# All D groups ahead of c1, and q weights of chunks 0 to 3 made by VectorE, in a three-layer interaction kernel

## The reference

```
z    = einsum('bid,bjd->bdij', base, curr)
curr = einsum('bdij,ijh->bhd', z, W_k) + b_k      # 100 outputs each
```

## Time and profile before

| | |
|---|---|
| device time, median of 3 runs | 185.86 us (185.47 to 185.96) |
| profiled execution: its time, its span from first to last instruction | 186.29 us, 184.5 us |
| PE matmul busy | 175.8 us (95% of the span) |
| DVE busy | 151.8 us (82%) |
| ACT busy | 73.9 us (40%) |
| POOL busy | 16.2 us (9%) |
| DMA moved | 37.71 MB, mean 204 GB/s |

### The profile page before, as it was taken

How to read it: one execution, slowest core, us unless ns; L and a number is a source line. 1 busy time by engine, 2 the same in 40 slices (tenths; PEclk the granted TensorE clock), 3 DMA queues, 4 the chain that set the end, 5 groups by cost and what they waited for, 6 DMA issues and landing times.

```text
span 184.5 us, 2573 instructions
## 1 busy us (share of the span) xinstructions
PE 175.8 (95%) x814; PEld 118.7 (64%) x814; DVE 151.8 (82%) x135; ACT 73.9 (40%) x79; POOL 16.2 (9%) x21
## 2 busy tenths in 40 slices
PE   7798998869999999999999999999999999999994
PEld 2364474546677777777777777777777777777760
DVE  0699698869999999999999999999999999300622
ACT  2554664124444624462446244534453445002001
POOL 3670010087000000000000000000000000000000
PEclk9999999999999999999999999999999999999999
DMA  6999997999797739774986597659765200000000
GB/s 192 379 409 411 412 219 218 231 406 397 230 324 233 234 122 321 247 227 124 331 230 228 126 322 235 223 135 329 228 219 128 99 0 0 0 0 4 0 0 0
DMA packets 11845, 37.71 MB, mean 204 GB/s; under 512 B 2305, under 2 KB 2941, under 8 KB 11838
## 3 DMA queue, kind: packets, MB, share of 16 engines
q1 hardware_dynamic: 11538, 37.38, 62.1%
q0 software_dynamic: 48, 0.16, 0.3%
q10 hardware_dynamic: 252, 0.09, 0.3%
HBM read 36.28 MB, written 1.33 MB: 204 GB/s over the span
## 4 chain that ended last, share of the span: by engine, by line
PE 79%; DMA 8%; SPq 3%; POOL 3%; issue 2%; DVE 1%; ACT 1%; DVEq 0%; ACTq 0%
PE q_ps L434 39%; PE c_ps L434 36%; DMA pair_sb<-d_dram 3%; DMA pair_sb<-w_pairs 3%; DMA d_dram<-w_d 2%; PE q_ps L518 2%; SPq L153 2%; POOL pair_sb L401 1%; POOL wq_low L424 1%; PE q_ps L443 1%; POOL wc_low L406 1%; DVE xb_z L246 1%; ACT z_high L324 1%; SPq L159 1%; PE c_ps L565 1%
## 5 line engine op out<-in xcount | busy, mean ns | idle before, releaser
L324 ACT ACTIVATE z_high<-xb_z 126x1024 fp32r<-126x1024 f32 x56 | 59.2, 1060 | 73.0 <-DVE xb_z L246 69.3
L253 DVE TENSOR_TENSOR z_low<-xb_z,z_high 126x1024 fp32r<-126x1024 f32 x56 | 68.9, 1232 | 1.1 <-ACT z_high L324 0.8
L246 DVE TENSOR_TENSOR xb_z<-x_a,xb_z 126x1024 f32<-126x1024 f32 x50 | 62.1, 1242 | 8.3 <-DMA xb_z<-xw 8.3
L434 PE MATMUL q_ps<-z_high,wq_high 126*101 126x512 f32 x108 | 34.1, 396 | 3.0 <-POOL wq_low L424 1.5
L434 PE MATMUL c_ps<-z_high,wc_high 126*101 126x512 f32 x112 | 35.5, 398 | 0.2 <-issue 0.2
L434 PE MATMUL c_ps<-z_high,wc_low 126*101 126x512 f32 x112 | 35.0, 394 | 0.0
L434 PE MATMUL c_ps<-z_low,wc_high 126*101 126x512 f32 x112 | 35.0, 394 | 0.0
L434 PE MATMUL q_ps<-z_high,wq_low 126*101 126x512 f32 x108 | 33.8, 394 | 0.0
L434 PE MATMUL q_ps<-z_low,wq_high 126*101 126x512 f32 x108 | 33.7, 393 | 0.0
L434 PEld LDWEIGHTS q_ps<-z_high,wq_high 126*101 126x101 f32 x108 | 17.7, 165 | 10.8 <-POOL wq_low L424 2.0
L434 PEld LDWEIGHTS c_ps<-z_high,wc_high 126*101 126x101 f32 x112 | 18.0, 165 | 9.0 <-issue 1.6
(11 more groups left out here) (56 smaller groups left out, 66.1 us busy)
## 6 DMA issues: line engine op xcount, KB each, us to landing
xb_z<-xw SPq DMA_DIRECT2D x50, 512.0 KB, 4.5
x_a<-xa SPq DMA_DIRECT2D x8, 512.0 KB, 5.0
w_d<-w2h SPq DMA_DIRECT2D x4, 512.0 KB, 7.4
w_post<-w1x SPq DMA_DIRECT2D x3, 512.0 KB, 10.0
d_dram<-w_d SPq DMA_DIRECT2D x4, 252.5 KB, 4.3
w_post<-w1x SPq DMA_DIRECT2D x1, 562.5 KB, 12.7
pair_sb<-d_dram SPq DMA_DIRECT2D x6, 82.9 KB
pair_sb<-w_pairs SPq DMA_DIRECT2D x1, 404.0 KB, 5.4
```

The costliest lines, as they stand in the source:

```text
L246: nc.vector.tensor_tensor(xb_z[0:K, c, :], x_a[0:K, u % 2, :], x_b, ALU.mult).then_inc(z_done, 1)
L253: nc.vector.tensor_tensor(z_low[0:K, m % SLOTS, :], xb_z[0:K, c, :], z_high[0:K, m % SLOTS, :].bitcast(fp32), ALU.subtract).then_inc(low_d ...
L324: nc.scalar.activation(z_high[0:K, m % SLOTS, :], xb_z[0:K, m % C, :], ACT.Copy).then_inc(high_done, 1)
L434: last = nc.tensor.matmul(ps[0:J, h * B:(h + 1) * B], w[0:K, c * J:(c + 1) * J], z[0:K, slot, h * B:(h + 1) * B], start=(c == 0 and k == 0 ...
```

## The change

PE does D groups 0 and 1, then `select_xb(6)`, then groups 2, 3 and 4, and all c1 chunks from 1 on after that. DVE copies groups 1 and 3 out of PSUM (around form(5)), ACT groups 0, 2 and 4. DVE makes the q weights of chunks 0 and 1 after split(9) of step m = 10, and those of chunks 2 and 3 after split(11) of step m = 12; POOL makes those of chunks 4 to 6 alone, on semaphores of its own. SP issues `load_xb(1, 2)` behind the gathers of piece 0 and `load_xb(1, 3)` behind all gathers.

```diff
-PREP_AT = 9
+PREP_AT = (10, 12)
...
@@ sync
-            sp.wait_ge(dgroup_copied, 2)
+            sp.wait_ge(dgroup_copied, 1)
+            sp.wait_ge(dgroup_copied_dve, 1)
...
-            sp.wait_ge(dgroup_copied, 4)
+            sp.wait_ge(dgroup_copied, 2)
+            sp.wait_ge(dgroup_copied_dve, 2)
...
-            sp.wait_ge(dgroup_copied, NG)
+            sp.wait_ge(dgroup_copied, 3)
             store_d(sp, 0, LEFT + 4 * GI, 4 * GI, LOWER - 4 * GI, d_stored)
-            sp.wait_ge(low_done, 3)
-            load_xb(1, 2)
             sp.wait_ge(equals_cleared, 1)
             sp.wait_ge(d_stored, 16 * DS)
             sp.wait_ge(d_stored_pool, 16)
             for side, t, piece in GATHER:
                 if piece == 1 and (side, t) == (0, 0):
-                    sp.wait_ge(low_done, 4)
-                    load_xb(1, 3)
+                    sp.wait_ge(low_done, 3)
+                    load_xb(1, 2)
                 if side == 0 or piece > 0:
                     gather_d(sp, side, t, piece)
-            for c in range(4, C):
+            for c in range(3, C):
                 sp.wait_ge(low_done, c + 1)
                 load_xb(1, c)
@@ vector
+            def copy_d(g):
+                dve.wait_ge(dgroup_done, g + 1)
+                nc.vector.tensor_copy(w2_d[:, g * GI * J:(g + 1) * GI * J], d_ps[g % 2]).then_inc(dgroup_copied_dve, 1)
+
-            def first_weights():
+            def first_weights(i):
...
                 for m in range(m0, m0 + BODY):
+                    if m == 5:
+                        copy_d(1)
                     form(it, m)
+                    if m == 5:
+                        copy_d(3)
...
-                    if m == PREP_AT:
-                        first_weights()
                     if m > 1:
                         split(it, m - 1)
+                    if m in PREP_AT:
+                        first_weights(PREP_AT.index(m))
@@ scalar
             copy_d(0)
-            copy_d(1)
             round_high(0, 4)
             copy_d(2)
-            copy_d(3)
             copy_d(4)
@@ gpsimd
-            for i in range(1, len(PREP_CUTS) - 1):
...
+            cols = slice(PREP_CUTS[2] * J, PREP_CUTS[3] * J)
+            pool.wait_ge(dpair_loaded[1], 16 * sum(g[2] == 1 for g in GATHER))
...
@@ tensor, q_chunk and d_group
-                if m in PREP_CUTS[:-1]:
+                if m in PREP_CUTS[:2]:
                     pe.wait_ge(wq_ready, PREP_CUTS.index(m) + 1)
+                if m == PREP_CUTS[2]:
+                    pe.wait_ge(last_ready, 1)
...
-                if g >= 2:
-                    pe.wait_ge(dgroup_copied, g - 1)
+                if g in (2, 4):
+                    pe.wait_ge(dgroup_copied, g // 2)
+                if g == 3:
+                    pe.wait_ge(dgroup_copied_dve, 1)
@@ tensor, the order
             d_group(0)
             d_group(1)
-            c1_chunk(0, 1)
+            select_xb(6)
             d_group(2)
             d_group(3)
-            select_xb(6)
             d_group(4)
-            for m in range(2, LAG):
+            for m in range(1, LAG):
                 c1_chunk(0, m)
```

More of the change, by code:

```diff
@@ L131, in build @@
         dgroup_done, dgroup_copied = sem("dgroup_done"), sem("dgroup_copied")
+        dgroup_copied_dve = sem("dgroup_copied_dve")
         wc_sums, wc_highs, wc_ready = sem("wc_sums"), sem("wc_highs"), sem("wc_ready")
         wq_sums, wq_highs, wq_ready = sem("wq_sums"), sem("wq_highs"), sem("wq_ready")
+        last_sums, last_highs, last_ready = sem("last_sums"), sem("last_highs"), sem("last_ready")
         filled, equals_cleared = sem("filled"), sem("equals_cleared")
@@ L273, in split_x @@
                                         ALU.subtract).then_inc(xa_split, 1)
-            def first_weights():
-                cols = slice(PREP_CUTS[0] * J, PREP_CUTS[1] * J)
-                dve.wait_ge(dpair_loaded[0], 16 * sum(g[2] == 0 for g in GATHER))
+            def copy_d(g):
+                dve.wait_ge(dgroup_done, g + 1)
+                nc.vector.tensor_copy(w2_d[:, g * GI * J:(g + 1) * GI * J], d_ps[g % 2]).then_inc(dgroup_copied_dve, 1)
+            def first_weights(i):
+                cols = slice(PREP_CUTS[i] * J, PREP_CUTS[i + 1] * J)
+                dve.wait_ge(dpair_loaded[i], 16 * sum(g[2] == i for g in GATHER))
                 nc.vector.tensor_tensor(q_sides[0:K, 0, cols], q_sides[0:K, 0, cols], q_sides[0:K, 1, cols],
                                         ALU.add).then_inc(wq_sums, 1)
-                dve.wait_ge(wq_sums, 1)
+                dve.wait_ge(wq_sums, i + 1)
                 nc.vector.tensor_copy(wq_high[0:K, cols], q_sides[0:K, 0, cols]).then_inc(wq_highs, 1)
-                dve.wait_ge(wq_highs, 1)
+                dve.wait_ge(wq_highs, i + 1)
                 nc.vector.tensor_tensor(wq_low[0:K, cols], q_sides[0:K, 0, cols], wq_high[0:K, cols].bitcast(fp32),
@@ L360, in _ @@
             copy_d(0)
-            copy_d(1)
             round_high(0, 4)
             copy_d(2)
-            copy_d(3)
             copy_d(4)
-            act.wait_ge(dgroup_copied, NG)
+            act.wait_ge(dgroup_copied, 3)
+            act.wait_ge(dgroup_copied_dve, 2)
             for m in range(5, BODY):
@@ L410, in _ @@
             pool.wait_ge(equals_cleared, 1)
-            pool.wait_ge(dgroup_copied, 4)
+            pool.wait_ge(dgroup_copied, 2)
+            pool.wait_ge(dgroup_copied_dve, 2)
             store_d(pool, 1, 0, UPPER - LEFT, LEFT, d_stored_pool, (0, 32))
-            for i in range(1, len(PREP_CUTS) - 1):
[L414 to L425, removed]
+            cols = slice(PREP_CUTS[2] * J, PREP_CUTS[3] * J)
+            pool.wait_ge(dpair_loaded[1], 16 * sum(g[2] == 1 for g in GATHER))
+            nc.gpsimd.tensor_tensor(q_sides[0:K, 0, cols], q_sides[0:K, 0, cols], q_sides[0:K, 1, cols],
+                                    ALU.add).then_inc(last_sums, 1)
+            pool.wait_ge(last_sums, 1)
+            nc.gpsimd.tensor_copy(wq_high[0:K, cols], q_sides[0:K, 0, cols]).then_inc(last_highs, 1)
+            pool.wait_ge(last_highs, 1)
+            nc.gpsimd.tensor_tensor(wq_low[0:K, cols], q_sides[0:K, 0, cols], wq_high[0:K, cols].bitcast(fp32),
+                                    ALU.subtract).then_inc(last_ready, 1)
         @block.tensor
```

## The result

The changed kernel takes 194.74 us (median of 4 runs, 193.88 to 195.04) against 185.73 us, a ratio of 1.048 (95% interval 1.044 to 1.052). The forecast was 194.9. The profiled execution took 194.78 us with a span of 193.0 us; the forecast for such an execution was 195.3 and 193.5.

The account below looks back on a forecast made before the run. PE bounds the kernel, so its idle time before the steady part counts fully. q 0 at 42.0 + 5.84 + 1.6 puts q 2 at 49.4 instead of 40.44; 185.86 + 9.0 = 194.9 us, range 191.5 to 197.3.

Parts of the forecast that it names:

- The bound, and the reorder of PE: PE sets the time from 60 to 169 us; idle before it counts one for one; the reorder costs nothing.
- DVE's copies: DVE's copies of groups 1 and 3 from PSUM: 0.65 us each, hidden in a 1.30 us wait; form(9) ready about 29.5.
- The stores: Last D store lands 0.4 us sooner, 27.64 instead of 28.04, out of nothing to about 0.8.
- The moved loads, the deciding step: Unit 1's chunks 2 and 3 load later, landing at 34.2 and 38.2; DVE waits before form(9) and form(10).
- The weights behind them: Weights of chunks 0 and 1 behind form(10) and split(9) are ready at 41.85; q 0 at 42.0 instead of 33.10.
- The pace: After PE's 10.9 us stop the clock falls; eight matmuls at 0.43 us, 3.5 us instead of 1.9, cost 1.6 us.
- the rival of 7 us: PE's slow pace after the stop lasts 7 us instead of 3.5: 1.6 us more, 196.5 us; chance 0.07.
- What I said of the second weights: DVE's weights of chunks 2 and 3, ready at 47.8, don't set q 2; the wait there is gone.
- The rival "not slower": Moved loads land in time for form(9) and form(10): +0.4 to +0.7, 186.3 to 186.6 us; chance 0.04.

Follow-up runs that it names:

- Loads back: Changed kernel with the loads of unit 1, chunks 2 and 3, issued where they stood before, all else kept: 189.98 us, ratio 1.021.
- both back and second weights at m = 10: Changed kernel with loads and weights of chunks 0 and 1 in old places, DVE making those of chunks 2 and 3 behind split(9): 185.52 us.
- D groups alone: Kernel before with only select 6 and groups 2 to 4 ahead of c1 1, groups 1 and 3 copied by DVE: 185.75 us, ratio 0.999.
- split(10) ahead: Kernel before with DVE making weights of chunks 2 and 3 at m = 10, POOL only 4 to 6, and split(10) ahead of those weights: 185.80 us.
- first weights back: Changed kernel with weights of chunks 0 and 1 made behind form(9), ahead of split(8), as before; loads stay late: 192.91 us, ratio 1.039.

## Why the prediction was right

**The bound, and the reorder of PE.** Right. Moving q 2 from 40.44 to 49.35 (8.9 us) moved the span by 8.5. The last 0.4 us came back behind q 2 (144.1 us to the end before, 193.0 - 49.35 = 143.65 now). The traces show where: q 2 to q 5 took 8.69 us before (40.44 to 49.13) and 8.29 now (49.35 to 57.64). Before, POOL's last range ran there beside DVE, whose instructions took up to 1.87 us, and now it was over; that this is the reason is not shown by a run. Group 3 waits a little for W1, as forecast, and the D groups' part alone makes no difference.

**DVE's copies.** 0.68 us each, 0.65 forecast; ready for form(9) at 29.5, as forecast (split(7) from 28.30).

**The stores.** The last one landed at 27.00, 1.04 us sooner, where I took 0.4 out of nothing to 0.8: under-sized here. In the other kernels with the same D part the gathers were issued from 27.13 to 28.02, and where the chain of waits shows W1's last part (it landed from 19.83 to 20.73) always 7.3 to 7.4 us behind it, as here (19.73 and 27.05). So most of that is how soon W1 happened to arrive. In the kernels with the old order of the D groups they were issued from 27.41 to 28.11.

**The moved loads, the deciding step.** Right: form(9) and form(10) wait for them, and both kernels that move just the loads, to or fro, change as they should. The landings were 5.6 and 9.9 us behind the last store (32.6 and 36.9), 6.6 and 10.53 forecast: the loads took 4.3 and 5.4 us from issue where I had copied 5.3 and 6.1 from the places before. With the earlier store form(10) starts at 37.00 instead of 38.3.

**The weights behind them.** Right in kind. split(9) cost 1.77 us to the next start (38.14 to 39.91), 1.3 forecast; the weights 1.06. q 0 at 41.11 instead of 42.0. The stop is 9.9 us, 10.9 forecast.

**The pace.** Right that the clock falls, and its price was under-sized: 8.24 - 5.84 = 2.4 us instead of 1.6, since the clock stayed at 1.2 GHz for 5.7 us behind the stop (41.11 to 46.8), not 3.5. That is halfway to the rival of 7 us, which priced it at 3.2. Filling the stop gives 1.9 us back. The two errors, -0.9 us at q 0 and +0.8 in the pace, cancel: q 2 was forecast at 49.4 and came at 49.35. That is luck: the forecast is closer than its terms were. There is a second piece of it: the profiled executions differ by 8.5 us (186.29 and 194.78), and the 9.0 fits the medians (185.73 and 194.74) because the profiled execution of before was some 0.5 us above its median and that of the changed kernel was not.

**What I said of the second weights was true and incomplete.** They were ready at 46.49, 5.4 us behind the start of q 0 (5.8 forecast), and set nothing, since PE came to q 2 at 49.35. But without the two other steps this place costs 5.5 us; the late q 0 hid it. The costs of the parts don't add up as independent terms: 2.4 us for the loads alone, 5.5 for the second weights, but 4.3 for the first and second weights together ("Loads back"). They are lateness on parallel ways to the same engine. The place of the first weights alone, in the kernel before, wasn't run.

**The rival "not slower"** (the loads land in time) was never near: the data of form(9) land 3.1 us behind the point where DVE wanted them, and those of form(10) at 36.9, where they would have had to be there before about 32.

## What to carry to other kernels

When an instruction is moved along an in-order engine, ask what it now stands behind: here two loads behind a chain of gathers, and then weights behind the instruction that waits for the load. Undoing one late step shows the next one; what a part costs alone can't be read from the whole.

Each version that shortened the 3.0 us of stops of the kernel before brought others back, of 0.75 to 1.6 us, mostly from a different cause (late low parts, weights made beside POOL, W1's arrival). When PE had to stop for 9.9 us, cheap matmuls into a free PSUM tile kept its clock.

## What was not expected of the hardware

- The clock can fall behind a stop as short as 1.54 us (low from about 33.7 to 37.1 in the kernel with both back and second weights at m = 10), while the kernel before passed two stops of 1.50 us at 1.00 in its profile, and two later kernels passed one of 1.59 (D groups alone) and one of 1.58 us (split(10) ahead) at 1.00 as well. So the length of the stop alone doesn't decide it. Of 29 other executions of the kernel before, run with the last group, six show a mean clock of 0.991 or less. The Trainium skill ("TensorE: Matmul & The Clock Gate", section "Part 1: The HAM clock gate") has the two levels, and the trace agrees with them.
- Behind a stop of 9.89 us PE kept working at the low level from 41.11 to about 46.8, 5.7 us, longer than the 3.5 us at the start of an execution. It doesn't follow the length of the stop either: 4.0 us behind a stop of 5.39 (loads back), 5.7 behind one of 3.46 (first weights back), and 3.5 behind the one of 1.54.
- DVE and POOL slow each other on these two-input instructions: DVE's subtraction of 1024 columns took 1.84 us instead of 1.22 beside POOL's of 303 columns (which took 1.71 us there, and 0.84 us in two other kernels, where DVE's product beside it took 1.86), and DVE's 1.08 us of weights grew to 2.4. The Trainium skill ("SBUF — State Buffer", section "SBUF: two separate sides") says that the two share a pair of ports that one instruction holds at a time; the rows agree in kind.
